# Quantised feed-forward: the largest product from a multiply-and-maximum pass, and 18 of 24 products formed in the last stage

## What is computed

```python
def act_qdq(x):
    qmax = 2.0 ** (ACT_BITS - 1) - 1.0
    scale = jnp.maximum(jnp.max(jnp.abs(x)) / qmax, 1e-12)
    return jnp.clip(jnp.round(x / scale), -qmax - 1.0, qmax) * scale
x = act_qdq(x)
up = act_qdq(x @ lpbq_dequant(w_up).T)
gate = act_qdq(x @ lpbq_dequant(w_gate).T)
sig = fixed_qdq_u16(jax.nn.sigmoid(gate))
gate = act_qdq(gate * sig)
o = act_qdq(gate * up)
return o @ lpbq_dequant(w_down).T
```

## Time and profile before

| | |
|---|---|
| time, median of 3 runs | 1730.08 us |
| lowest and highest | 1728.72 and 1730.42 us |
| the profiled execution, time | 1731.12 us |
| its span, first to last instruction | 1729.4 us |
| mean granted TensorE clock | 0.953 of full speed |
| PE busy | 1539.9 us, 89% of the span |
| DVE busy | 968.1 us, 56% |
| ACT busy | 830.9 us, 48% |
| POOL busy | 465.1 us, 27% |

### The profile page before, as it was taken

The page is one execution under the profiler, slowest core; times in us unless marked ns, Lnnn a source line. Parts: engine busy times, 40 slices in busy tenths (PEclk is TensorE's granted clock), DMA queues, the critical chain, the costliest instruction groups (busy, mean ns, idle before and its releaser), DMA issues. The chain is left out here.

```text
span 1729.4 us, 26863 instructions
## 1 busy us (share of the span) xinstructions
PE 1539.9 (89%) x10059; PEld 1073.7 (62%) x10059; DVE 968.1 (56%) x2224; ACT 830.9 (48%) x1821; POOL 465.1 (27%) x582
## 2 busy tenths in 40 slices
PE   6999999998887889999998999999999779992099
PEld 3777776666655667877876466666656534441088
DVE  3665767856766434222222666766755445699932
ACT  4455665563565322212112566566666423797730
POOL 3222233343435210000004555555433100241000
PEclk9999999998999989999998999999999879996599
DMA  3440111011241154334335111110000000001111
GB/s 112 163 151 7 43 33 50 27 36 53 64 121 50 47 163 136 110 121 153 110 96 146 37 38 50 50 49 17 23 13 13 13 13 0 1 0 39 58 37 62
DMA packets 100912, 108.30 MB, mean 63 GB/s; under 512 B 25394, under 2 KB 89788, under 8 KB 100784
## 3 DMA queue, kind: packets, MB, share of 16 engines
q1 hardware_dynamic: 94640, 90.01, 16.6%
q0 software_dynamic: 6144, 16.57, 3.0%
HBM read 64.77 MB, written 42.01 MB: 62 GB/s over the span
## 5 line engine op out<-in xcount | busy, mean ns | idle before, releaser
L1740 POOL TENSOR_SCALAR c_pr<-c_pr,c_rsum 128x256 f32<-128x256 f32 x256 | 127.2, 512 | 189.5 <-DVE c_rsum L2046 189.1
L1961 ACT ACTIVATE c_pr<-bank,c_nmax 128x256 f32<-128x256 f32 x256 | 117.7, 472 | 118.1 <-DVE c_nmax L2041 118.0
L1511 ACT ACTIVATE b_G<-bank 128x320 f32<-128x320 f32 x128 | 55.9, 437 | 210.3 <-PE bank L1461 210.3
L1461 PE MATMUL bank<-b_XT,shared 128*128 128x320 f32 x512 | 154.0, 435 | 0.0
L1475 PE MATMUL bank<-shared,b_G 128*128 128x256 f32 x640 | 142.2, 379 | 0.0
L2041 DVE TENSOR_REDUCE c_nmax<-bank 128x2 f32<-128x512 f32 x128 | 82.4, 686 | 105.7 <-PE bank L1791 102.5
L1475 PEld LDWEIGHTS bank<-shared,b_G 128*128 128x128 f32 x640 | 120.9, 190 | 17.8
L1060 DVE TENSOR_TENSOR hT_all<-bank,a_causal 128x512 f32<-128x512 f32 x128 | 79.4, 683 | 65.7 <-PE bank L557 65.7
L492 POOL TENSOR_TENSOR a_L<-a_L,a_Lm 128x1232 f32<-128x1232 f32 x32 | 71.9, 2248 | 163.9 <-DVE a_Lm L1075 163.9
L1461 PEld LDWEIGHTS bank<-b_XT,shared 128*128 128x128 f32 x512 | 92.1, 192 | 27.3 <-issue 0.8
L1530 DVE COPY b_Y<-bank 128x256 f32<-128x256 f32 x80 | 34.0, 425 | 120.3 <-PE bank L1475 120.1
(11 more groups left out here) (325 smaller groups left out, 3397.7 us busy)
## 6 DMA issues: line engine op xcount, KB each, us to landing
shared<-L_ffn_w SPq DMA_DIRECT2D x32, 512.0 KB, 6.0
t_slots_in<-a_h SPq DMA_DIRECT2D x20, 512.0 KB, 6.8
shared<-t_slots_in SPq DMA_DIRECT2D x15, 640.0 KB, 7.1
t_slots_out<-b_Y SPq DMA_DIRECT2D x15, 640.0 KB, 4.1
hT_all<-x SPq DMA_DIRECT2D x8, 512.0 KB, 4.0
a_xr<-x SPq DMA_DIRECT2D x8, 512.0 KB, 3.8
t_x_a<-a_x SPq DMA_DIRECT2D x8, 512.0 KB, 2.8
shared<-t_x_a SPq DMA_DIRECT2D x8, 512.0 KB
```

The lines of the kernel that those rows point to most:

```text
L1461: t = p.matmul(P[2 + n % 2][:, 0:HC], w1[e % 3][:, u, 128 * f:128 * f + 128], XT[e % 2][:, u, HC * m:HC * m + HC], start=(u == 0), stop=(u ...
L1740: p.tensor_scalar(pr[k][:, e, u, :], pr[k][:, e, u, :], rsum[k][:, e, u:u + 1], 1.0, ALU.mult, ALU.mult).then_inc(q.pr_ready, 1)
L1961: a.activation(pr[t % 2][:, e, u, :], P[e][:, S * u:S * u + S], ACT.Exp, bias=nmax[t % 2][:, e, u:u + 1], accum_out=sums[t % 2][:, e, u:u ...
```

## The change

- The kept tiles (`PRODUCT_KEPT`: 0, 1, 2 and the three of the banks) are treated as before: product into `raw`, then a magnitude, which now follows in the same turn. Their activation integers are made by DVE, two turns ahead.
- For the other 18 tiles ACT writes magnitudes of the integers (`ACT.Abs`), and DVE runs one `tensor_tensor_reduce`: it multiplies, takes the maximum of the row into `cur["o"]`, and writes the products to a scratch (`unread`) that nobody reads. Each waits for the one before.
- The turns are in the order `IN_TURN`, one kept tile in four.
- In the last stage, ACT makes the integers of those 18 tiles again, with their signs (from `up` or `hT`, and from the activations that still stand in `raw`), DVE forms scale times product as int16 in one of four rooms (`o_room`, `scalar_tensor_tensor`) and scales it back into `raw`, in place. The kept tiles take one ACT pass and the scaling. The first group goes in four pieces of 128 tokens.
- PE reads `raw`. DVE scales one tile after each of a group's first three additions.
- The residual's rooms now lie over eight tiles of `up`, and five of its loads wait until the tile there has been read a second time; they stand in SP's queue between the stores.

The core of the diff:

```diff
-        of = [pair(up[:, NG * NT * D:NG * NT * D + FC * T]), pair(hT[:, 0, 0:FC * T])]
-        oi = [pair(hT[:, 1, FC * T // 2 * k:FC * T // 2 * k + FC * T // 2].bitcast(I16)) for k in range(2)]
-        PIECES = [(0, 0, 128), (0, 128, 128), (0, 256, 256)] + [(g, 0, T) for g in range(1, NG)]
-        LEAD = 3
+        FT = FC // 2
+        PRODUCT_KEPT = (0, 1, 2) + IN_BANKS
+        IN_TURN = (0, 3, 4, 5, 1, 6, 7, 8, 2, 9, 10, 11, 19, 12, 13, 14, 20, 15, 16, 17, 22, 18, 21, 23)
+        turn_of = {n: r for r, n in enumerate(IN_TURN)}
+        A_ON_DVE = (0, 1, 2, 19, 20, 22)
+        later = [n for n in range(FT, NTILE) if n not in IN_BANKS]
+        o_room = [hT[:, k, T * (NG - 1):T * NG].bitcast(I16) for k in range(2)]
+        o_room += [spare[:, W:W + T].bitcast(I16), wuT[:, :, :].rearrange("p c n -> p (c n)")[:, W:W + T].bitcast(I16)]
+        unread = hT[:, :, T * (NG - 1):T * NG]
+        X_ROOM = (0, 1, 2, 3, 6, 9, 12, 10)
...
             def _(s):
-                s.wait_ge(q.ui_ready, NG * NT * D // W)
-                for g in range(NG):
+                for g in range(3):
+                    s.wait_ge(q.ui_ready, turn_of[X_ROOM[g]] + 1)
                     s.dma_start(xin[g], x_rows[g]).then_inc(arrived[g], 16)
                 for g in range(NG - 1):
+                    if g + 3 < NG:
+                        s.wait_ge(q.ui_again, later.index(X_ROOM[g + 3]) + 1)
+                        s.dma_start(xin[g + 3], x_rows[g + 3]).then_inc(arrived[g + 3], 16)
                     s.wait_ge(q.y_ready, NT * (g + 1))
                     s.dma_start(out_rows[g], xin[g]).then_inc(q.y_out, 16)
...
-                        p.wait_ge(q.of_ready, g + LEAD if g else min(j, 2) + 1)
+                        p.wait_ge(q.of_ready, NT + FT * g if g else j + 1)
...
-                            t = p.matmul(P[n % 8][:, 0:D], of[g % 2][:, f, 128 * j:128 * j + 128], wdT[:, f, :], start=(f == 0), stop=(f == FC - 1))
+                            t = p.matmul(P[n % 8][:, 0:D], raw[:, f, T * g + 128 * j:T * g + 128 * j + 128], wdT[:, f, :], start=(f == 0), stop=(f == FC - 1))
...
+                        x = a.activation(pair(u_room[r % NI]), up_tile(n), ACT.Copy if n in PRODUCT_KEPT else ACT.Abs, scale=inv["u"][:, :])
                     x.then_inc(q.ui_ready, 1)
+                    if n not in A_ON_DVE + A_ON_POOL:
...
+                        a.activation(pair(a_room[r % NI]), tile(n), ACT.Copy if n in PRODUCT_KEPT else ACT.Abs,
+                                     scale=inv["a"][:, :]).then_inc(q.ai_ready, 1)
...
                 a.wait_ge(q.scaled, 5)
+                for j in range(NT):
+                    a.activation(pieces(o_room[j]), raw[:, :, 128 * j:128 * j + 128], ACT.Copy, scale=inv["o"][:, :]).then_inc(q.oi_ready, 1)
+                for n in range(FT, NTILE):
+                    if n in IN_BANKS:
+                        a.wait_ge(q.of_ready, n + 1 - FT)
+                        a.activation(pair(o_room[(n + 1) % NO]), tile(n), ACT.Copy, scale=inv["o"][:, :]).then_inc(q.oi_ready, 1)
+                    else:
+                        k = later.index(n)
+                        if k >= NI:
+                            a.wait_ge(q.o_again, k - NI + 1)
+                        a.activation(pair(u_room[k % NI]), up_tile(n), ACT.Copy, scale=inv["u"][:, :]).then_inc(q.ui_again, 1)
+                        a.activation(pair(a_room[k % NI]), tile(n), ACT.Copy, scale=inv["a"][:, :]).then_inc(q.ai_again, 1)
...
+                def a_integers(n):
+                    r = turn_of[n]
+                    if r >= NI:
+                        v.wait_ge(q.prod_ready, r - NI + 1)
+                    v.tensor_scalar(pair(a_room[r % NI]), tile(n), inv["a"][:, :], None, ALU.mult).then_inc(q.ai_first, 1)
...
+                    if n in PRODUCT_KEPT:
+                        v.tensor_tensor(tile(n), pair(a_room[r % NI]), pair(u_room[r % NI]), ALU.mult).then_inc(q.prod_ready, 1)
+                    else:
+                        v.wait_ge(q.prod_ready, r)
+                        v.tensor_tensor_reduce(unread, pair(a_room[r % NI]), pair(u_room[r % NI]), 1.0, 0.0, ALU.mult, ALU.max,
+                                               cur["o"][:, n:n + 1]).then_inc(q.prod_ready, 1)
...
+                a_integers(0)
+                for r, n in enumerate(IN_TURN):
                     product(n)
-                    if n == 0:
+                    if r == 0:
                         make_unit("o", (scale["a"][:, :], scale["u"][:, :]))
-                    if n:
-                        product_magnitude(n - 1)
-                product_magnitude(NTILE - 1)
+                    product_magnitude(n)
+                    if r + 2 < NTILE and IN_TURN[r + 2] in A_ON_DVE:
+                        a_integers(IN_TURN[r + 2])
...
+                def scale_piece(j):
+                    v.wait_ge(q.oi_ready, j + 1)
+                    v.tensor_scalar(raw[:, :, 128 * j:128 * j + 128], pieces(o_room[j]), scale["o"][:, :], None, ALU.mult).then_inc(q.of_ready, 1)
+
+                def scale_tile(n):
+                    room = pair(o_room[(n + 1) % NO])
+                    if n in IN_BANKS:
+                        v.wait_ge(q.oi_ready, NT + IN_BANKS.index(n) + 1)
+                    else:
+                        k = later.index(n)
+                        v.wait_ge(q.ui_again, k + 1)
+                        v.wait_ge(q.ai_again, k + 1)
+                        v.wait_ge(q.of_ready, n + 1 - FT)
+                        v.scalar_tensor_tensor(room, pair(a_room[k % NI]), inv["o"][:, :], pair(u_room[k % NI]), ALU.mult, ALU.mult).then_inc(q.o_again, 1)
+                        v.wait_ge(q.o_again, k + 1)
+                    v.tensor_scalar(tile(n), room, scale["o"][:, :], None, ALU.mult).then_inc(q.of_ready, 1)
+
+                for j in range(NT):
+                    scale_piece(j)
+                for n in range(FT, 2 * FT):
+                    scale_tile(n)
                 for g in range(NG):
                     v.wait_ge(arrived[g], 16)
                     for j in range(NT):
                         n = NT * g + j
                         v.wait_ge(q.y_psum, n + 1)
                         v.tensor_tensor(xin[g][:, j, :], P[n % 8][:, 0:D], xin[g][:, j, :], ALU.add).then_inc(q.y_ready, 1)
-                    if g + 2 < NG:
-                        scale_back(g + LEAD + 1)
+                        if j < FT and g + 2 < NG:
+                            scale_tile(FT * (g + 2) + j)
```

More of the change, by code:

```diff
@@ L2230, in unit_bank, with pieces @@
             return P[m] if m < 4 else P[(m + 1) % 8] if m < NU - 2 else P[m - NU + 5]
+        def pieces(room):
+            return room[:, 0:128 * FC].rearrange("p (f t) -> p f t", t=128)
         def up_tile(n):
@@ L2260, in feed_forward @@
                             "gi_ready sig_ready sq_ready act_ready act_part ui_ready ai_first ai_ready prod_ready prod_part "
-                            "oi_ready of_ready y_psum y_ready y_out "
+                            "ui_again ai_again o_again oi_ready of_ready y_psum y_ready y_out "
                             + " ".join(f"xf_in{g}" for g in range(NG)))
@@ L2380, in _ @@
                 a.wait_ge(q.scaled, 3)
-                for n in range(NTILE):
-                    if n >= NI:
-                        a.wait_ge(q.prod_ready, n - NI + 1)
+                for r, n in enumerate(IN_TURN):
+                    if r >= NI:
+                        a.wait_ge(q.prod_ready, r - NI + 1)
                     if n in IN_BANKS:
                         for m in (2 * n, 2 * n + 1):
-                            x = a.activation(u_room[n % NI][:, T * (m % 2):T * (m % 2) + T], unit_bank(m)[:, :], ACT.Copy, scale=inv["u"][:, :])
+                            x = a.activation(u_room[r % NI][:, T * (m % 2):T * (m % 2) + T], unit_bank(m)[:, :], ACT.Copy, scale=inv["u"][:, :])
@@ L2387, in _ @@
                     else:
-                        x = a.activation(pair(u_room[n % NI]), up_tile(n), ACT.Copy, scale=inv["u"][:, :])
+                        x = a.activation(pair(u_room[r % NI]), up_tile(n), ACT.Copy if n in PRODUCT_KEPT else ACT.Abs, scale=inv["u"][:, :])
                     x.then_inc(q.ui_ready, 1)
-                    if n:
-                        if n == 1:
+                    if n not in A_ON_DVE + A_ON_POOL:
+                        if r == 1:
                             a.wait_ge(q.scaled, 4)
-                        a.activation(pair(a_room[n % NI]), tile(n), ACT.Copy, scale=inv["a"][:, :]).then_inc(q.ai_ready, 1)
+                        a.activation(pair(a_room[r % NI]), tile(n), ACT.Copy if n in PRODUCT_KEPT else ACT.Abs,
+                                     scale=inv["a"][:, :]).then_inc(q.ai_ready, 1)
@@ L2395, in _ @@
                 a.wait_ge(q.scaled, 5)
-                for n, (g, at, width) in enumerate(PIECES):
-                    if g >= 2:
-                        a.wait_ge(q.of_ready, n - 1)
```

(18 more changed lines are left out.)

32 lines of the change are left out of this document (16 added, 16 removed).

## The result

| | before | changed |
|---|---|---|
| median of 5 runs | 1729.95 us | 1719.58 us |
| lowest to highest | 1728.72 to 1730.42 us | 1717.25 to 1722.24 us |
| the profiled execution, time | 1731.12 us | 1720.90 us |
| its span | 1729.4 us | 1719.2 us |
| from ACT's first up pass to d_top_o | 57.34 us | 45.54 us |

The ratio of the runs is 0.9935, 95% interval 0.9924 to 0.9947: faster by 0.65%, forecast 0.67%.

What follows compares the result with a forecast made beforehand. DVE was taken to bound the product stage and PE the last stage. With ACT as new bound, d_top_o comes 11.8 us earlier: 1731.12 becomes 1719.3, less 1.04 for the median gives 1718.3 us; range 1717.0 to 1727.0.

Steps and rivals of the forecast that it cites:

- The chain of two stages: Feed-forward's end: product stage set by DVE, then last stage set by PE; d_top_o comes 11.8 us earlier.
- ACT as the new bound: Product stage: ACT's 39 passes at 1.04 us and three at 1.16, together 44.1 us, set its length.
- The table load: Product stage, ACT: 1.28 us, paid in full if the magnitude function is not in the loaded set; chance 0.07.
- d, the fused pass: Product stage, DVE: duration of one multiply-and-maximum pass, taken as 1.3 us, between 1.22 and 1.42.
- d + 0.04: Product stage, DVE: step between fused passes, their duration plus a 0.04 us gap for waiting on the one before.
- The half-speed rival: Product stage, DVE: fused pass takes two cycles an element, 2.28 us, making the kernel slower, at 1735 us; chance 0.08.
- DVE as the bound: Product stage: DVE still sets it if the fused pass exceeds 1.43 us; 1723 us at 1.7; chance 0.10.
- the crossing at d = 1.43: Product stage: fused-pass duration in us at which DVE's block of four turns equals ACT's 7.28 us.
- the first rival: Product stage: DVE remains the bound, stage 18.1 + 18d from 1580.35 us, d being the fused pass's duration; chance 0.10.
- Order and rooms: Product stage: walking 24 turns with three rooms for integers, ACT waits for DVE in no turn.
- The last stage: After d_top_o: PE covers the moved work; second 512 tokens ready at 11.8 us, slack 3.4; DVE 7.4 of 10.36 us.
- SP: Residual loads: three go in the product stage, five wait ahead of output stores, with time to spare; cost nothing.

Runs made afterwards that it cites:

- e7: Changed kernel with only the order of turns altered, so the kept tiles stand together: product stage 51.01 us against 45.54, profiled time 1717.12 us.
- e3: Changed kernel with each of the 18 products formed twice in the last stage: PE's last stage 89.86 us against 85.05, profiled time 1724.69 us.
- e9: Changed kernel plus 28 spare PE products before the scale chain and five after the peak is spread: last stage 83.15 us, time 1701.21 us.
- e10: Changed kernel plus 30 spare PE products before the scale chain, one inside, six after: last stage 83.04 us, median 1701.15 us, ratio 0.9919 to the kernel before.
- e5: Changed kernel plus 28 spare PE products from the 17th up tile on, before the scale chain: last stage 85.78 us, time 1700.56 us.
- e6: Changed kernel plus 10 spare PE products from the 20th up tile on, before the scale chain: last stage 85.76 us, time 1710.02 us.

## Why the prediction was right

**The chain of two stages.** Held. d_top_o came 45.54 us after ACT's first pass, 45.6 was forecast; the gain of the stage is 11.80 us, 11.8 was forecast.

**ACT as the new bound, 39 passes of 1.04 and three of 1.16.** Held: its last pass starts 42.93 us after its first, 43.0 by the sum. That ACT loses nothing by the magnitude function was taken from a sigmoid's row, and the row was right (1138 against 1134 ns). The table load did not come. The Trainium skill (ScalarE: Activation LUTs, on table sets) has abs in every set; the trace agrees.

**d, the fused pass.** Taken as 1.3 between 1.22 and 1.42. Measured 1.22, the lower end: the read is an instruction of its own, but at 0.08 us it overlaps the pass, so d is not in the upper part of the interval. The mis-sized term is the gap behind it: two fused passes in a row start 1.39 apart (1586.59 and 1587.98), not d + 0.04 = 1.34, because the next waits for the read and 0.17 beyond. Where another pass stands between, there is no such gap. The second fused pass, and the two kept products that bound a block in which DVE waits for nothing of ACT's:

```profile
1587.98 1.23 DVE L2509 CUSTOM_DVE_ANT_0 hT_all<-d_gate_int,d_sig_int 128x1024 f32<-128x1024 int16 x1 [0.17 <-DVE d_cur_o L2509]
...
1590.94 1.22 DVE L2506 TENSOR_TENSOR d_raw<-d_gate_int,wgT 128x1024 f32<-128x1024 int16 x1
...
1597.69 1.22 DVE L2506 TENSOR_TENSOR d_raw<-d_gate_int,d_sig_int 128x1024 f32<-128x1024 int16 x1
```

The block takes 6.75 us; 6.9 was forecast, against 7.28 of ACT. The two errors are small and in opposite directions, and as ACT was the bound neither reached the time. The half-speed rival fell, and so did DVE as the bound: over six blocks it has some 3 us in hand (2.3 by the forecast), as its waits for ACT, 2.8 us in all, also say. That was not much, and which side of the crossing at d = 1.43 the pass would fall was not known beforehand: by an estimate from these rows, an accumulator read of 0.2 us behind each pass, instead of 0.08 that overlaps it, would have put DVE's block at 7.3, level with ACT's. The forecast had some luck there. Two slips in the working change nothing: the sum of the first rival, 18.1 + 18 x 1.7 from 1580.35, gives 1629.05 and not 1628.9; and the remark that DVE's relief would have been "far more" than 11.8 does not fit the prediction's own sums, by which DVE alone goes from 55.7 to 18.1 + 18 x 1.3 = 41.5 us, 14.2 less.

**Order and rooms.** The prediction said in half a sentence that ACT would wait for DVE in no turn. It did not; e7 shows that in another order it would have, and that the half sentence held up 5.5 us of the 11.8.

**The last stage.** The second group was to be ready 11.8 us after the scale: its last scaling ends at 1641.02, 11.8 after 1629.21. The forming pass was 60 ns longer than the nearest row, DVE's step from it to the scaling 1.32 instead of 1.26. Cover per group: 3 us forecast, e3 agrees.

**SP.** Five loads now stand between the stores; no wait for a load shows on DVE.

**The total.** 1718.3 was forecast, the median is 1719.58, 1.3 us more. In the profiled execution the stages gave the 11.8 (and 1.1 by the clock, which was luck), and 2.67 us were lost in front, where the prediction had no term; the cause of that stays open. On the other chip the medians give 7.8 us of gain, 4.0 less than forecast: that the total came out within 1.3 us is in part luck, that the product stage did is not. The range, 1717.0 to 1727.0, was wide upward for a slow fused pass that did not come, and its lower end was too near: it took only the spread of three runs, 1.7 us, while five runs of the changed kernel spread over 5.0.

## What to carry to other kernels

Before sizing what a lighter engine will give, write down the second engine's own sum for the stage: here DVE's relief was worth 11.8 us and not the 14.2 of DVE's own sum in the prediction's terms, and 5.2 of the 11.8 came only because ACT was relieved in the same edit. When two engines end within some 3 us of each other, the order of heavy and light turns counts as much as the sums (5.5 us here), and further shifting pays little. Read such a change by the length of the stage that it changes: the product stage, which ACT and DVE set, repeats to 0.02 us, while the last stage varies by 1.35 us with PE's clock and the whole time by up to 10.

## What the runs showed of the hardware

- A DVE pass that multiplies two int16 tensors, writes f32 and keeps the maximum takes as long as the product alone: 1220 ns for 1024 elements a partition, and its accumulator read is a second instruction of 82 ns. The Trainium skill (VectorE: DVE Perf Modes, the section on two Vector instructions with no wait between them) says that such an operation is two instructions; the trace agrees. The rule of half throughput that was a rival here (the Trainium skill, Vector Engine (DVE) Microarchitecture Reference, the section on points that are easy to get wrong) shows neither on this pass nor on the int16 scale-multiply-multiply (1278 ns): the measurement decides.
- PE given spare products before and inside the scale chain of 3.7 to 3.9 us starts the next stage at 2.4 GHz (granted clock 1.00, e9 and e10) instead of 1.2 (0.50), which was worth 1.7 to 3.1 us of an 86 us stage. Kept busy only up to the chain (e5, e6) it gained nothing in that stage, but the chain itself took 3.70 us instead of 4.01.
- One program's time varied by 10 us on one chip (1713.72 to 1723.79), without any change in it.
